# Joining the expert rows of the last stage: two groups added by VectorE, the third fetched plainly and added by GpSimd

## The reference, cut to what matters

```python
xn = _layernorm(x)
x = x + _L1_attn_ref(xn, ...) + _L1_ffn_ref(xn, gate_w, expert_w, expert_b)

# _L1_attn_ref, its end
normed = (out - mean) * rsqrt(var + GN_EPS) * gn_weight + gn_bias
attn = einsum('btd,ed->bte', normed, Wo)

# _L1_ffn_ref: each token goes through its best two of eight experts
top_w, top_i = top_k(xf @ gate_w.T, 2);  top_w = softmax(top_w)
y = einsum('td,edo->eto', xf, expert_w) + expert_b
out = sum over the token's two experts e of top_w[e] * y[e]
```

## Time and profile before

| | |
|---|---|
| median of 3 runs | 434.31 us (433.55 to 435.04) |
| the profiled execution's own time | 432.89 us |
| its span, first to last instruction | 431.2 us |
| granted TensorE clock, mean | 0.994 |
| PE busy | 417.8 us (97%) |
| DVE busy | 344.7 us (80%) |
| ACT busy | 184.1 us (43%) |
| POOL busy | 171.6 us (40%) |
| DMA, mean | 109 GB/s |

### The profile page before, as it was taken

One profiled execution on the slowest core, in us unless ns is written; L12 is line 12 of the kernel. 1 busy time (PEld: TensorE's weight loads), 2 busy tenths in 40 slices (PEclk: granted clock), 3 DMA queues, 4 the chain that ended last, 5 costly groups with the idle time before them and its releaser, 6 DMA issues.

```text
span 431.2 us, 7440 instructions
## 1 busy us (share of the span) xinstructions
PE 417.8 (97%) x2488; PEld 364.1 (84%) x2488; DVE 344.7 (80%) x1087; ACT 184.1 (43%) x361; POOL 171.6 (40%) x200
## 2 busy tenths in 40 slices
PE   7999999999999999999999999999999999899993
PEld 5788888978899989878898988788889888799882
DVE  6799998898997778889977689899877766478682
ACT  4745554443263546333617252524362343524130
POOL 1556469631045102510245625001620165356556
PEclk9999999999999999999999999999999999999997
DMA  8992799950011310000021300000204744322289
GB/s 272 406 321 90 221 277 283 272 149 0 2 45 54 97 52 2 0 2 1 24 75 51 98 2 0 3 0 2 98 2 125 219 123 137 111 77 83 75 220 278
DMA packets 30373, 46.87 MB, mean 109 GB/s; under 512 B 2696, under 2 KB 24480, under 8 KB 29824
## 3 DMA queue, kind: packets, MB, share of 16 engines
q1 hardware_dynamic: 25984, 35.75, 27.6%
q0 software_dynamic: 3360, 9.85, 7.8%
q10 hardware_dynamic: 992, 0.81, 0.6%
HBM read 22.74 MB, written 23.65 MB: 108 GB/s over the span
## 4 chain that ended last, share of the span: by engine, by line
PE 82%; DVE 10%; issue 3%; POOL 2%; ACT 1%; DMA 1%; POOLq 0%; DVEq 0%; ACTq 0%
PE D L711 25%; PE G L711 22%; PE U L711 21%; PE M L711 7%; PE D L742 1%; DVE mid_lo L1370 1%; PE M L861 1%; DVE mid L1493 1%; DVE rows L1507 1%; POOL sums_gate L660 1%; DVE carry_gain L1731 1%; DMA rows<-x 1%; PE M L836 1%; DVE gamma L1733 1%; PE M L734 1%
## 5 line engine op out<-in xcount | busy, mean ns | idle before, releaser
L711 PE MATMUL D<-w_hi,mid_hi 128*128 128x256 f32 x260 | 74.1, 285 | 0.1
L711 PE MATMUL D<-w_hi,mid_lo 128*128 128x256 f32 x260 | 73.6, 283 | 0.0
L711 PE MATMUL D<-w_lo,mid_hi 128*128 128x256 f32 x260 | 73.5, 283 | 0.0
L1112 ACT ACTIVATE mid<-G 128x512 f32<-128x512 f32 x64 | 37.8, 595 | 71.9 <-PE G L711 45.9
L1507 DVE SCALAR_TENSOR_TENSOR rows<-D,weight,rows 128x256 f32<-128x256 f32 x128 | 54.0, 477 | 8.4 <-PE D L711 4.5
L1493 DVE TENSOR_TENSOR mid<-mid,U 128x512 f32<-128x512 f32 x64 | 42.7, 684 | 21.1 <-ACT mid L1112 10.6
L551 POOL TENSOR_TENSOR w_lo<-w_raw,w_hi 128x512 fp32r<-128x512 f32 x35 | 50.4, 1471 | 23.0 <-ACT w_hi L1081 12.2
L1081 ACT ACTIVATE mid_hi<-mid 128x512 fp32r<-128x512 f32 x64 | 39.9, 632 | 38.1 <-DVE mid L1493 36.6
L1370 DVE TENSOR_TENSOR mid_lo<-mid,mid_hi 128x512 fp32r<-128x512 f32 x64 | 49.1, 787 | 4.9 <-ACT mid_hi L1081 3.3
L711 PEld LDWEIGHTS D<-w_hi,mid_hi 128*128 128x128 f32 x260 | 49.8, 191 | 1.7 <-issue 0.9
L711 PE MATMUL G<-xT_hi,w_hi 128*128 128x512 f32 x126 | 50.4, 400 | 0.3 <-POOL w_lo L551 0.3
(11 more groups left out here) (369 smaller groups left out, 956.4 us busy)
## 6 DMA issues: line engine op xcount, KB each, us to landing
sorted_rows<-weighted SPq DMA_DIRECT2D x8, 1542.0 KB, 19.4
stage<-sorted_rows SPq DMA_DIRECT2D x31, 128.5 KB, 2.1
w_raw<-weights SPq DMA_DIRECT2D x2, 1280.0 KB, 14.4
w_raw<-weights SPq DMA_DIRECT2D x2, 1024.0 KB, 23.0
rows<-x SPq DMA_DIRECT2D x7, 256.0 KB, 3.2
w_raw<-weights SPq DMA_DIRECT2D x2, 768.0 KB, 8.8
part<-rows SPq DMA_DIRECT2D x12, 128.0 KB, 2.2
sums_gate<-part SPq DMA_DIRECT2D x3, 512.0 KB, 5.2
```

Of the source, the lines that this page charges most:

```text
L711: ins = nc.tensor.matmul(out_ap, a, b, start=(first and n == 0), stop=(last and n == 3 * len(pairs) - 1))
L1112: nc.scalar.activation(mid[:, c, :], GU[2 * c][:, :], ACT.Silu).then_inc(silu_ready, 1)
```

## The change

It is in four parts.

1. The third group (index 2, `JOINS`) no longer has an adding DMA. Its first region is fetched plainly by SyncE into a new tile `fetched[3]`, the first of now four plain loads; then come the second regions of groups 2, 0, 1. GpSimd issues two adding DMAs, for groups 0 and 1.
2. GpSimd adds `fetched[3]` to `sums_of[2]` in two halves (`add_first`) between the joins and `att_low(3)`, and `fetched[2]` in two halves (`add_second`) after `att_low(3)`.
3. VectorE adds `fetched[0]` and `fetched[1]` in four halves. They stand in `result(3)`: one after the first tile's add, one after the second's, two after the fourth's. SyncE stores group 2 first, then groups 0 and 1.
4. The scatter of unit 4 waits also until seven unit products are done; unit 5's condition is the same as before.

```diff
+JOINS = LAST - 1
+SUMS_BEHIND = ((0,), (1,), (), (2, 3))
...
             sp.wait_ge(made_stored, 16 * PIECES)
-            for g in range(LAST):
+            sp.dma_start(fetched[LAST], side_by_side(returned, SPARE + JOINS * GT)).then_inc(fetched_rows[LAST], 16)
+            for g in (JOINS, *range(JOINS)):
                 sp.dma_start(fetched[g], side_by_side(returned, SPARE + REGION + g * GT)).then_inc(fetched_rows[g], 16)
-            for n in range(2 * LAST):
-                g, pair = n // 2, slice(2 * (n % 2), 2 * (n % 2) + 2)
-                sp.wait_ge(summed, n + 1)
+
+            def store_sum(g, half):
+                pair = slice(2 * half, 2 * half + 2)
                 sp.dma_start(side_by_side(out, g * GT)[:, pair, :], sums_of[g][:, pair, :]).then_inc(stored, 16)
+
+            for half in range(2):
+                sp.wait_ge(pool_summed, half + 1)
+                store_sum(JOINS, half)
+            for n in range(2 * JOINS):
+                sp.wait_ge(vector_summed, n + 1)
+                store_sum(n // 2, n % 2)
...
-                if u == 5:
-                    pool.wait_ge(unit_ps, 8)
+                if u in (4, 5):
+                    pool.wait_ge(unit_ps, u + 3)
...
+            def add_first(half):
+                pair = slice(2 * half, 2 * half + 2)
+                pool.wait_ge(part_loaded[JOINS], 16)
+                pool.wait_ge(fetched_rows[LAST], 16)
+                nc.gpsimd.tensor_tensor(sums_of[JOINS][:, pair, :], sums_of[JOINS][:, pair, :], fetched[LAST][:, pair, :],
+                                        ALU.add).then_inc(first_summed, 1)
...
             pool.wait_ge(made_stored, 16 * PIECES)
-            for g in range(LAST):
+            for g in range(JOINS):
                 join(g)
+            for half in range(2):
+                add_first(half)
             att_low(LAST)
-            for n in range(2 * LAST):
-                add_fetched(n)
+            for half in range(2):
+                add_second(half)
...
+            def add_fetched(n):
+                g, pair = n // 2, slice(2 * (n % 2), 2 * (n % 2) + 2)
+                dve.wait_ge(joined[g], 16)
+                dve.wait_ge(fetched_rows[g], 16)
+                v.tensor_tensor(sums_of[g][:, pair, :], sums_of[g][:, pair, :], fetched[g][:, pair, :], ALU.add)\
+                    .then_inc(vector_summed, 1)
...
                     v.tensor_tensor(rows[g % 2][:, t, :], rows[g % 2][:, t, :], proj_at(g, t), ALU.add)\
                         .then_inc(result_ready, 1)
+                    if g == LAST:
+                        for n in SUMS_BEHIND[t]:
+                            add_fetched(n)
```

More of the change, by code:

```diff
@@ L195, in build @@
         fetched = [over(f"fetched{g}", *PAIRS_AT[g], D, TILES)[:, :].rearrange("p (t d) -> p t d", t=TILES)
-                   for g in range(LAST)]
+                   for g in range(LAST + 1)]
         att = ln[:, :, :].rearrange("p (c b) t -> p c b t", c=KC)
@@ L357, in build @@
         made_stored = sem("made_stored")
-        joined = [sem(f"joined{g}") for g in range(LAST)]
-        fetched_rows = [sem(f"fetched_rows{g}") for g in range(LAST)]
-        summed = sem("summed")
+        joined = [sem(f"joined{g}") for g in range(JOINS)]
+        fetched_rows = [sem(f"fetched_rows{g}") for g in range(LAST + 1)]
+        first_summed = sem("first_summed")
+        pool_summed = sem("pool_summed")
+        vector_summed = sem("vector_summed")
         tokens_made = sem("tokens_made")
@@ L654, in join, with add_second @@
                     .then_inc(joined[g], 16)
[L656 to L661, removed]
+            def add_first(half):
[4 more added lines that the diff above has]
+                                        ALU.add).then_inc(first_summed, 1)
+            def add_second(half):
+                pair = slice(2 * half, 2 * half + 2)
+                pool.wait_ge(fetched_rows[JOINS], 16)
+                pool.wait_ge(first_summed, half + 1)
+                nc.gpsimd.tensor_tensor(sums_of[JOINS][:, pair, :], sums_of[JOINS][:, pair, :], fetched[JOINS][:, pair, :],
+                                        ALU.add).then_inc(pool_summed, 1)
             for g in range(GROUPS):
```

## The result

| | time, median | range | profiled execution | its span |
|---|---|---|---|---|
| before | 433.78 us | 433.09 to 435.04 (6 runs) | 432.89 us | 431.2 us |
| after | 430.6 us | 429.55 to 431.13 (6 runs) | 430.42 us | 428.7 us |

The ratio is 0.9929, with an interval of 0.9911 to 0.9946: 3.1 us less.

A forecast was written before the change was run, and what follows sets the result against it. GpSimd's adds and full DMA engines were taken to bound the tail equally. DMA bound 430.05 and engine order 430.2 gave a span of 430.1, 1.1 us less than 431.2, scatter 0: time 433.2 us, range 431.3 to 435.2.

The forecast's parts named there:

- two chains end together: Kernel's end: GpSimd's adds and the DMA transfers finish together, so taking away one alone would bring little.
- the tail: From the last scatter's landing near 411.1 us to the end: span 430.1 instead of 431.2, 1.1 us less.
- The order of the engines: Kernel's end: VectorE's order is late next, giving a span of 430.2, transfers close behind at 430.05.
- A sum of mine: Loads after 416 us: adding DMAs end near 423.4 and plain ones near 423.6, at 0.13 MB a microsecond each.
- I take 0: Unit 4's scatter, moved from 366.93 to near 370.3: no effect assumed; possible gain up to 1.25 us, cost up to 3.2.
- rival B: Near 367 to 370 us: ScalarE's 3.22 us stall goes with unit 4's scatter; -2.35 us, about 432.0; chance 0.18.
- My argument against it: Unit 4's scatter: nothing in the trace says it causes ScalarE's 3.22 us stall, since earlier scatters pass without it.
- my signs of being wrong: Among them: the span up to TensorE's last expert pair, which ended at 420.24, moves by over 0.5 us.
- 434.31: Assumed median of the kernel before, in us, to which the difference of the spans was carried over.
- D: ScalarE's copies at 370 to 373 us: moved scatter stalls them, 3.2 us; +2.1 net, time 436.4; chance 0.16.
- the clash: Projection's end: VectorE's first half-group add waits beside GpSimd's second pair of adds, 0.8 us taken, between 0 and 1.1.

The follow-up runs named there:

- e3: From e2: all three groups joined by adding DMAs again, three plain loads, VectorE adding groups 0 and 1, GpSimd group 2 after att_low; 0.9996 of before.
- e4: From e2: same transfers (two adding DMAs, four plain loads), but GpSimd does all adds, two before att_low and six after, VectorE none; 1.0005 of before.
- e2: The changed kernel with unit 4's further wait taken out again, so only the end of groups 0 to 2 is changed; 0.998 of before.
- r1_before: The kernel before, unedited, run again beside before on a chip where that takes 429.75 us; ratio 0.9999.
- r4_tail_only: The changed kernel without unit 4's further wait, timed again on a chip where before takes 433.09 us; 0.9964 of before.
- groups 3 and 5: Follow-up runs on one chip: variants of GpSimd's first adds (before 433.12 us), then unit 4's wait alone and the tail alone (before 433.09 us).

## Why the prediction was wrong, point by point

**Right: two chains end together.** Neither half of the tail moves the time (e3 0.9996, e4 1.0005), both do (e2 0.998).

**Right, its size in part: the tail.** I had an end 18.98 us behind the issue of the first load (430.1 less 411.12). Five of the seven profiles of this very tail took between 18.77 and 19.01; the two whose loads were issued earliest behind the router's product (34.7 us, the others 35.5 to 37.5), and in which shift_g was caught, took 19.3 and 20.02. As a gain in time, against my 1.1 us, the tail gave 0.8 to 0.95 on two chips and 1.55 on the third. That the figure for the first comparison is so close is partly luck, for some terms shift against each other:
- The first load lands 3.6 us behind its issue, not 4.1; GpSimd starts 0.15 later. Its adds, 1.27 each, ended 6.3 us behind the issue; I had 6.7.
- TensorE waits 0.40 us, not 0.26.
- VectorE's first half-group add takes 1.38, not 1.49; the later ones 0.68.
- The last store is issued 5.7 us behind the projection's start, not 6.5, yet the end is 4.1 us further and not 3.2, for the DMA engines are full to 427. The order of the engines is not late next, as I wrote; the transfers are, by about a microsecond (my 2.7 us from the last issue to its landing and 0.5 to the end would have given 427.8, and the span is 428.7).
- A sum of mine was a little short: at 0.13 MB a microsecond each, 1.04 and 0.99 MB end at 424.0 and 423.6, not at 423.6 and 423.4.

**Wrong: "I take 0" for unit 4's scatter.** This is the failed step. Where the kernel before takes 433 us, as in the first comparison and in my profile, moving it is worth 0.9958, 1.8 us (1.2 to 2.5 by the interval), more than the 1.25 that I gave rival B; where the rest lies was not traced. B names the mechanism that happened, and I gave it 0.18. My argument against it was that earlier scatters pass without a stall; but the row with the stall lay in front of me, TensorE had no slack, and the place was the only one that the change touched there. One of my signs of being wrong came with it: the span up to TensorE's last expert pair is 1.8 us shorter (418.46 against 420.24). As a difference, my tail and the measured scatter give 1.1 + 1.8 = 2.9 us, of 3.1 to 3.3 measured; the tail itself is worth 1.55 us where before takes 433 (1.0 to 2.2 by the interval) and 0.8 to 0.95 elsewhere. In absolute time there are 0.5 us more: I carried the difference to 434.31, and the kernel before ran at 433.78 beside the one after.

**Did not happen: D.** Unit 4's and unit 5's scatters now follow each other from 370.37 on, and ScalarE's longest wait up to 376 us is 1.69, a fraction of the stall D needed; the router's products behind it come earlier than before, not later.

**Not foreseen:** that GpSimd's first adds can catch VectorE's short operations. I looked for the clash only at the half-group adds.

**Open.** Why the stall is there on one chip and in the first comparison, and not on the two other chips. Whether the scatter's own work carries it or GpSimd's being busy: the run for it fell on a chip without one. By what way it reaches ScalarE, whose product was done at 367.4. One rival was not tested: that ScalarE waits for its own instructions. A packet of an instruction queue starts just before the stall, shown here for 365 to 366 us of the kernel before, then of r1_before (packets, MB, share of 16 engines):

```profile
q14 instruction: 1, 0.01, 6.4%
```
```profile
q14 instruction: 1, 0.01, 1.9%
```

As shares of 16 us of engine time these are 1.02 and 0.31 us. r4_tail_only, which stalls too, has 6.3%, 1.01 us; in the profiles without the stall it takes 0.31 to 0.93 us. No view tells whose instructions they are.

The fastest kernel is the changed one. The one that waits for the gains can't be told from it (0.9921, interval 0.9903 to 0.994, against 0.9925).

## What to carry to other kernels

Where a step that the change moves lies beside an unexplained stall on the critical path, give the loss of that stall as much chance as its staying, and look at the trace of a second chip where there is one. Where two chains end together, change both at once, and expect an experiment on either alone to show nothing. Before long GpSimd operations that read SBUF are put into a gap, look for short VectorE operations with two SBUF inputs in the same microseconds: each can wait for a whole GpSimd operation (1.15 to 1.22 us instead of 0.16 here). And before two stretches of two profiles are compared, see that both begin at the same distance from a common event; here 1.1 us of difference between first load and end was an earlier first load.

## What the runs showed that I had not expected

- The same kernel takes 433.1 to 433.8 us in groups 3 and 5 and the first comparison, and 429.5 to 430.3 in the others, the mean granted clock being 0.991 to 0.997 in the one kind and 0.993 to 0.998 in the other. Part of it is ScalarE starting late on finished products: the 3.15 to 3.22 us of idle time near unit 4's scatter, and in r4_tail_only another, 1.8 us behind transposes that ended at 394.1:

```profile
395.89 0.60 ACT L1102 ACTIVATE w_hi<-M 128x512 fp32r<-128x512 f32 x1 [2.98 <-remote]
```

- A VectorE operation on 128x4 values takes 1.15 to 1.22 us instead of 0.16 beside a GpSimd add of 1.28 to 1.30 us.
- Loads beside adding DMAs keep the rates read before the change: 0.50 and 0.61 MB in 414 to 418 us, 0.54 and 0.57 in 418 to 422, as the earlier trace rows had 0.54 and 0.52. Queues of the kernel after, 418 to 422 us (packets, MB, share of 16 engines):

```profile
q0 software_dynamic: 147, 0.54, 67.2%
q1 hardware_dynamic: 155, 0.57, 37.8%
```
